# When two engines read the registers that choose the expert weights: once per tile, or all of a phase at its first tile

## The reference

```python
x = x + layernorm(attn(layernorm(x)))     # x: 8 batches of 512 tokens of 128 numbers, float32
x = x + layernorm(ffn(layernorm(x)))
# attn: mix each token with the one before it, times W_in, relu, a decaying running sum
#       along the sequence, times W_out
# ffn:  a gate picks 2 of 8 experts for each token; the 8192 (token, expert) pairs are sorted by expert;
#       for each pair  layer_3 = (silu(h @ w0[e]) * (h @ w1[e])) @ wo[e],  w0, w1: 128 x 512, wo: 512 x 128
#       the two results of a token are weighted by a softmax of their gates and added
```

## Time and profile before

| what | value |
|---|---|
| median of 3 runs | 271.58 us (270.92 to 273.17) |
| the profiled execution | 271.02 us, of which the instructions span 269.2 us |
| mean granted TensorE clock | 0.966 of full speed |
| TensorE busy (matmul) | 242.1 us, 90% of the span |
| VectorE busy | 184.7 us, 69% |
| ScalarE busy | 180.0 us, 67% |

### The profile page before, as it was taken

The page is one execution under the profiler, slowest core; times in us unless marked ns, Lnnn a source line. Parts: engine busy times, 40 slices in busy tenths (PEclk is TensorE's granted clock), DMA queues, the critical chain, the costliest instruction groups (busy, mean ns, idle before and its releaser), DMA issues.

```text
span 269.2 us, 8125 instructions
## 1 busy us (share of the span) xinstructions
PE 242.1 (90%) x2071; PEld 230.2 (86%) x2071; DVE 184.7 (69%) x811; ACT 180.0 (67%) x521; POOL 167.3 (62%) x190
## 2 busy tenths in 40 slices
PE   6977847899999999999999999999999999999800
PEld 2745726899999999999999999999999999999700
DVE  4678997877756876776678677843434334998754
ACT  3176775677778768696776678656566565668592
POOL 3317773786787878877788877775324233277740
PEclk9999995999999999999999999999999999999965
DMA  6999972313421321331132123323232209302048
GB/s 172 289 322 369 358 222 54 81 41 84 121 70 43 99 73 39 84 92 51 45 89 82 42 71 92 110 87 95 75 92 56 62 19 358 159 18 97 13 152 234
DMA packets 29676, 31.70 MB, mean 118 GB/s; under 512 B 4779, under 2 KB 22189, under 8 KB 29505
## 3 DMA queue, kind: packets, MB, share of 16 engines
q1 hardware_dynamic: 24448, 22.56, 27.8%
q0 software_dynamic: 4320, 8.50, 9.1%
q10 hardware_dynamic: 864, 0.13, 0.3%
HBM read 19.58 MB, written 12.05 MB: 117 GB/s over the span
## 4 chain that ended last, share of the span: by engine, by line
PE 79%; DVE 11%; DMA 3%; issue 2%; ACT 2%; DVEq 1%; SPq 0%; POOL 0%; POOLq 0%
PE bank L1763 47%; PE bank L1800 24%; PE bank L1758 3%; PE bank L1714 2%; DVE sb_early L1002 2%; DMA sb_gate_w<-in_L_ffn_gate_kernel 1%; DMA sb_early<-pair_rows 1%; PE bank L1664 1%; DVE sb_x L1017 1%; DVE sb_stats L948 1%; DVE sb_rest_stats L978 1%; PE bank L1682 1%; DMA pair_rows<-sb_y_rows,sb_y_pair 1%; PE bank L1690 1%; ACT sb_square L647 1%
## 5 line engine op out<-in xcount | busy, mean ns | idle before, releaser
L1763 PE MATMUL bank<-sb_xeT,sb_w_now 128*128 128x128 f32 x1136 | 140.5, 277 | 0.0
L1763 PEld LDWEIGHTS bank<-sb_xeT,sb_w_now 128*128 128x128 f32 x1136 | 134.4, 194 | 0.5 <-issue 0.3
L527 POOL DMA_INDIRECT pair_rows<-sb_y_rows,sb_y_pair x71 | 74.6, 1050 | 51.3 <-ACT sb_y_rows L771 30.3
L1369 DVE TENSOR_TENSOR sb_gated<-bank,sb_silu 128x512 f32<-128x512 f32 x71 | 48.9, 689 | 59.1 <-PE bank L1763 51.6
L514 POOL DMA_INDIRECT expert_rows<-sb_row,sb_place x64 | 64.4, 1006 | 30.1 <-issue 16.4
L1800 PE MATMUL bank<-sb_w_raw,sb_gated 128*128 x568 | 75.4, 276 | 0.1
L1800 PEld LDWEIGHTS bank<-sb_w_raw,sb_gated 128*128 128x128 f32 x568 | 69.1, 192 | 0.3 <-issue 0.2
L742 ACT ACTIVATE sb_silu<-bank 128x512 f32<-128x512 f32 x71 | 42.3, 595 | 17.4 <-PE bank L1763 17.4
L737 ACT ACTIVATE sb_xeT<-bank 128x128 f32<-128x128 f32 x71 | 19.5, 274 | 44.4 <-PE bank L1758 43.5
L760 ACT ACTIVATE sb_w_now<-sb_w_raw 128x512 f32 x71 | 44.3, 624 | 0.4 <-issue 0.4
L1388 DVE COPY sb_w_now<-sb_w_raw 128x512 f32 x71 | 30.1, 424 | 1.4 <-issue 1.4
(11 more groups left out here) (204 smaller groups left out, 252.5 us busy)
## 6 DMA issues: line engine op xcount, KB each, us to landing
sb_taken_rows<-expert_rows SPq DMA_DIRECT2D x71, 65.5 KB, 1.9
sb_w_raw<-in_L_ffn_w SPq DMA_DIRECT2D x2, 2048.0 KB, 16.4
sb_pairs_early<-pair_rows SPq DMA_DIRECT2D x3, 1024.0 KB, 6.9
out_dram<-sb_x SPq DMA_DIRECT2D x3, 512.0 KB, 3.2
pair_rows<-sb_y_rows,sb_y_pair POOLq DMA_INDIRECT x71, 2.3
sb_x<-in_L_attn_x SPq DMA_DIRECT2D x4, 256.0 KB, 4.1
sb_pairs_early<-in_x_turned SPq DMA_DIRECT2D x4, 256.0 KB, 4.5
sb_pairs_early<-in_x_turned SPq DMA_DIRECT2D x1, 1024.0 KB, 8.0
```

Of the source, the lines that this page charges most:

```text
L527: pool.indirect_dma_start(pair_rows[:, :], bass.IndirectOffsetOnAxis(ap=y_pair[group % 2][:, t % PAIRS:t % PAIRS + 1], axis=0), y_rows[slo ...
L1369: dve.tensor_tensor(gated[t % 2][:], p_l2[:], silu[t % 2][:], ALU.mult).then_inc(c["gated"], 1)
L1763: last = pe.matmul(to[:, n * P:(n + 1) * P], w[:, n * P:(n + 1) * P], x, start=True, stop=True)
```

## The change

`chunk_of` on ScalarE and on VectorE no longer reads one register a call. At the first tile of a phase, behind the wait for that phase's table, it reads the registers of all tiles of the phase, one after the other; for the other tiles it does nothing. The number of reads stays 71 on each engine. TensorE's own `chunk_of` and SP's reads of row numbers are as they were.

```diff
@@ ScalarE
                 for p in range(PHASES + 1):
                     if t == first_tile(p):
                         act.wait_ge(s_table, p + 1)
-                chunks[t] = act.value_load(tile_chunk_i[0:1, t:t + 1], min_val=0,
-                                           max_val=(E - 1) * FC)
+                        for n in tiles_of_phase(p):
+                            chunks[n] = act.value_load(tile_chunk_i[0:1, n:n + 1], min_val=0,
+                                                       max_val=(E - 1) * FC)
@@ VectorE
                 for p in range(PHASES + 1):
                     if t == first_tile(p):
                         dve.wait_ge(s_table, p + 1)
-                chunks[t] = dve.value_load(tile_chunk_i[0:1, t:t + 1], min_val=0,
-                                           max_val=(E - 1) * FC)
+                        for n in tiles_of_phase(p):
+                            chunks[n] = dve.value_load(tile_chunk_i[0:1, n:n + 1], min_val=0,
+                                                       max_val=(E - 1) * FC)
```

## The result

The changed kernel takes 314.73 us (median of 4 runs, 310.29 to 316.85) against 271.28 us before: ratio 1.147, 95% interval 1.135 to 1.160. Forecast were 314 us in a range of 301 to 327. Medians here are of all runs, while the ratios and intervals leave out the slow ones, among them 316.48 and 316.85 us of this kernel and 869 us of `batch_2`; by its two other runs the change costs 40 us. Its profiled execution took 312.97 us with a span of 311.1, so the span is 41.9 us longer than before.

A forecast was written before the change was run, and what follows sets the result against it. TensorE was taken to bound the kernel, without gaps in the tile loop. Waits of 33.2 us plus 3.2 and 6.4 us of lower clock made 42.8 us on the profiled 271.0: 313.8, rounded to 314 us, range 301 to 327.

The forecast's parts named there:

- What bounds the kernel: Tile loop: TensorE is busy 60.00 of 60.00 us, so reads taken out of ordinary slots gain 0.
- What one read costs: Reads in a row on ScalarE and VectorE: one after the other, 0.55 and 0.62 us each.
- Rival C: Reads in a row overlap and cost 0.28 us each; 282 to 286 us in all; chance 0.07.
- Rival D: Not slower: reads hide behind the waiting of ScalarE and VectorE; 271 us; chance 0.03.
- The slots of the phases: Seven added reads in slots 7 to 39 stall TensorE 3.72 us each; 22 in slot 47 stall it 12.0.
- The sum of the waits: TensorE's waits over the whole kernel: 18.6 + 1.9 + 12.0 + 0.7 = 33.2 us.
- The terms ahead of the loop: Two added VectorE reads on the path to the running sum, less slot 0's removed read: net 0.7 us.
- for slot 2: Four added reads in slot 2, 2.48 us less the cover of 0.62: 1.9 us of wait.
- The clock: Lower clock behind TensorE's waits: 3.2 us lost for slot 47, 6.4 for two of five small stalls; chance 0.52.
- Rival B: The clock falls after each of the six stalls, 6 x 3.2 us: 323.4 us; chance 0.18.
- Rival A: The clock falls for slot 47 alone, 3.2 us: 307.4 us; chance 0.18.
- The range: Whole kernel, 301 to 327 us: the forecast, rivals A and B with the bounds of a read's cost.

The follow-up runs named there:

- `batch_2`: Kernel before, with ScalarE and VectorE each reading two registers at every second tile of a phase: 275.97 us, ratio 1.016.
- `no_read`: Kernel before, with the register reads of ScalarE and VectorE replaced by a constant, expert 0's place: 270.00 us, ratio 0.994.
- the halves: Kernel before with only one engine reading a phase's registers at once: ScalarE alone 301.98 us (ratio 1.111), VectorE alone 318.75 us (ratio 1.172).
- `stalls_filled`: Changed kernel, with TensorE doing matmuls of ones into an idle bank in the slots that stall: 304.53 us, ratio 1.119 against the kernel before.
- `full_change`: The changed kernel run once more, on the chip of the one-engine kernels with filled gaps: 311.74 us, ratio 1.139 against the kernel before.
- `act_only`: Kernel before, with ScalarE alone reading a phase's registers at its first tile, VectorE one a slot as before: 301.98 us, ratio 1.111.

## Why the prediction was right

*What bounds the kernel.* TensorE did, and reads in ordinary slots were free or nearly so: `no_read` wins 0.4 to 0.9%. Right.

*What one read costs.* 0.61 us on VectorE and 0.55 on ScalarE, one after the other, forecast 0.62 and 0.55. Rival C, overlapping reads, is out. Rival D, that the reads hide, is out with it.

*The slots of the phases.* Forecast were 3.72 us of wait in each of five slots, and 12.0 in slot 48; with the clock kept up they are 3.8 to 3.9 and 12.2. ScalarE's wait was forecast as 2.5 and then 1.2; in slot 32 the profile has 2.46 and 0.79. The second looks shorter because the profile counts from the end of the first eight matmuls, while the forecast gave them 0.89 us from start to start; counted that way it is 163.20 - 161.28 - 0.89 = 1.03. In slots 24 and 40 the clock fell as the first layer began, and no second gap is left: matmuls that run slower fill it. The prediction took the multiplication of slot 31 as released by its read, though its row names a matmul; waits within 0.2 us of the forecast say that the two ended close together. That the two engines read side by side is shown by the halves, which don't add up.

*The sum of the waits.* Forecast 33.2 us; `stalls_filled` is 0.119 x 271.3 = 32 us above the kernel before, its own stretch of lower clock ahead of slot 3 included. The terms ahead of the loop, 0.7, and for slot 2, 1.9, are the least settled. TensorE's wait for the running sum grew from 0.98 to 1.90 us, and the reads of slot 2 cost 0.40 us of wait in slot 3:

```profile
50.12 1.73 PE L1716 MATMUL bank<-sb_w_out_wide,sb_early 128*128 128x136 f32 x8 [1.90 <-DVE sb_early L1003]
...
57.15 1.13 PE L1765 MATMUL bank<-sb_xeT,sb_w_now 128*128 128x128 f32 x8 [0.40 <-DVE sb_gated L1370]
```

In the profile of `full_change` these waits are 2.90 us and, in slot 3, 0.68 and 1.03. The profiles have different stretches of lower clock there, and the start of the changed kernel was not tried by itself. All that lies ahead of slot 5 came to 4.2 us in the one profile and 2.4 in the other, where 2.6 were forecast.

*The clock.* This is the term that came near its size by luck. I had three slow stretches of 3.2 us lost, 9.6 in all, with two of five small stalls among them. The profile has one behind each of the five, and each lasts about 3.4 us instead of 6.8 (one of five lasts 6.7 in `full_change`). Set against `stalls_filled` slot by slot, the five lose 5.2 us and slot 48 another 1.8; by the ratios the runs put the loss at 5 to 8 us. Too few stretches were counted, each too dear. A small part of that is a slip in the working: 3.40 us runs from the first start to the last end and 1.79 from start to start; the like of 3.40 is the 1.95 of the earlier trace rows, which makes 2.9 us of the 3.2. Rival B, that each stall brings one, was right in the count and wrong in the time, for it took 6.8 us for each. Rival A fell: in slots 8, 24 and 40 a single gap of 2.44 to 2.56 us was enough. The rule of the Trainium skill that goes with it, page "TensorE: Matmul & The Clock Gate", section "Why this matters for your kernels", names gaps above about 3 us as what to avoid; the changed kernel's profile disagrees, with gaps of 2.43 to 2.56 in all five slots and the clock at 0.50 behind them (in slots 16 and 32 after a second gap of 0.8), and `act_only` agrees in four of its five slots. What decides in a single case between none, 3.4 and 6.8 us of lower clock stays open.

*The range.* Rivals A and B spanned 307 to 323, and the runs of the two sets lie at 309 to 317. In the profiled execution, whose span grew by 41.9 us where 42.8 were forecast, the errors partly cancel: the five slots and slot 48 with 19.2 and 12.2 us of waits (from `stalls_filled`; forecast 18.6 and 12.0) and all ahead of slot 5 with 4.2 (2.6) came out higher, the clock with 7.0 (9.6) lower. By the ratios the change costs only 38 to 40 us, so that 314 lies within 1 us of the median of 314.73 is partly luck: two of the four runs were near 316.5.

## What to carry to other kernels

In this kernel a register read is work of the engine's sequencer, and it holds up everything that stands behind it on that engine; spread over slots it sits beside running instructions and costs next to nothing, and gathered into one place it costs its full length less the slack of that one slot. Before batching such small steps, look for the idle time that they are meant to remove: where the bounding engine has none, there is next to nothing to win, and the slack has to be read slot by slot, at the busiest slot too, not at one. When a change stalls TensorE, count the clock behind the stall as a second cost, and keep the engine busy with idle matmuls to see the two apart.

## What had not been expected

A second engine's delay made the kernel faster: with VectorE's reads alone gathered it takes 318.75 us, with ScalarE's gathered as well 311.74 and 314.73. ScalarE's delay holds back the first layer, so that the wait of 3.48 us falls apart into 2.46 and 0.79 with work between, and the stretches at the lower clock shrink from 6.8 us (four of five) to 3.4 (nine of ten in the two profiles); with the gaps filled the difference is gone (305.96 against 304.53). So the difference is clock; that the parting of the gap is what shortens the stretches is the likeliest reading, but was not tried by itself.
